# Delta rule: idle slots rebalanced, four banks for output transposes, first gathers ahead of constants, ranking without zero products

## The reference

```python
# x: (16, 512, 256)
x = layernorm(x + linear_attention(x))            # 1
x = layernorm(x + top2_of_8_experts(x))           # 2
x = layernorm(x + delta_rule_layer(x))            # 3
x = layernorm(x + composed_mlp(x))                # 4

def delta_rule_layer(x):                          # 4 heads, keys of 64, values of 128
    h = rmsnorm(layernorm(x, ln1_g, ln1_b), rms_in_w)
    q, k, v = (silu(conv4(h @ W)) for W in (Wq, Wk, Wv))      # causal, by channel
    q, k = l2norm(q) / 8, l2norm(k)
    g, beta = -exp(A_log) * softplus(h @ Wa + dt_bias), sigmoid(h @ Wb)
    for t in range(512):                          # state S: keys x values, per head
        S = S * exp(g[t])
        S = S + outer(k[t], (v[t] - k[t] @ S) * beta[t])
        o[t] = q[t] @ S
    o = rmsnorm(o, o_norm_w) * silu(h @ Wg)
    x = x + o @ Wo
    return gelu(layernorm(x, ln2_g, ln2_b) @ W2 + b2) + x

def composed_mlp(x):          # W1, W2: sums of the 32 best of 64 low-rank products
    return gelu(x @ W1) @ W2  # W1 = sum_k w_k A_k B_k, the same for W2
```

## Time and profile before

| | |
|---|---|
| three runs | 4705.86, 4717.77, 4723.58 us; median 4717.77 |
| profiled execution | 4709.05 us, its span 4707.4 us |
| busy share of the span | PE 86%, PEld 67%, DVE 53%, ACT 42%, POOL 22% |
| mean granted clock of PE | 0.907 of full speed |
| delta rule, 2080 to 4225 us | 2145 us, 46% of the span |
| mlp stages (experts, last) | PE 9 tenths busy in nearly every slice |

### The profile page before, as it was taken

How to read it: one execution, slowest core, us unless ns; L and a number is a source line. 1 busy time by engine, 2 the same in 40 slices (tenths; PEclk the granted TensorE clock), 3 DMA queues, 4 the chain that set the end, 5 groups by cost and what they waited for, 6 DMA issues and landing times. The chain is left out here.

```text
span 4707.4 us, 72598 instructions
## 1 busy us (share of the span) xinstructions
...
## 2 busy tenths in 40 slices
...
DMA packets 220431, 345.98 MB, mean 73 GB/s; under 512 B 99956, under 2 KB 171380, under 8 KB 201972
## 3 DMA queue, kind: packets, MB, share of 16 engines
...
...
## 5 line engine op out<-in xcount | busy, mean ns | idle before, releaser
L539 ACT ACTIVATE moe_rel<-moe_fc 128x512 f32<-128x512 f32 x284 | 169.6, 597 | 798.7 <-PE moe_fc L504 798.7
L504 PE MATMUL moe_fc<-moe_xT,moe_win 128*128 128x256 f32 x2272 | 504.0, 380 | 1.5 <-issue 0.8
L515 PE MATMUL moe_o<-moe_wout,moe_hT 128*128 128x256 f32 x2272 | 502.0, 379 | 0.0
L504 PEld LDWEIGHTS moe_fc<-moe_xT,moe_win 128*128 128x128 f32 x2272 | 432.9, 191 | 61.2 <-issue 2.1
L515 PEld LDWEIGHTS moe_o<-moe_wout,moe_hT 128*128 128x128 f32 x2272 | 426.3, 190 | 55.1
L563 DVE TENSOR_TENSOR moe_hT<-moe_rel 128x512 f32<-128x512 f32 x284 | 196.6, 692 | 366.5 <-ACT moe_rel L539 366.5
L1781 DVE SCALAR_TENSOR_TENSOR gdr_y<-gdr_bank,gdr_cw,gdr_y 128x511 f32<-128x511 f32 (+2 forms) x384 | 287.5, 749 | 52.6 <-ACT gdr_y L2045 29.0
L2242 PE MATMUL gdr_bank<-gdr_hT,gdr_wqkv 128*128 128x512 f32 x512 | 282.5, 680 | 21.3 <-ACT gdr_qk L2060 15.8
L572 DVE COPY moe_osb<-moe_o 128x512 f32<-128x512 f32 x71 | 49.1, 692 | 424.9 <-PE moe_o L515 424.9
L2361 PE MATMUL gdr_bank<-gdr_ident,gdr_T 128*128 128x128 f32 x768 | 132.5, 301 | 126.5 <-DMA gdr_T<-blocks_in 76.0
L693 PE MATMUL ffn_fc<-ffn_xT,ffn_win 128*128 128x512 f32 x512 | 224.0, 596 | 2.0 <-DMA ffn_win<-ffn_w 2.0
...
## 6 DMA issues: line engine op xcount, KB each, us to landing
...
```

The lines of the kernel that those rows point to most:

```text
L504: ins = nc.tensor.matmul(fc_ps[j][:, m % 2, :], win[u][:, c, m * P:(m + 1) * P], xT[:, c, :], start=(c == 0), stop=(c == DT - 1))
L515: ins = nc.tensor.matmul(o_ps[u][:, t, :], hT[u][:, k, t * P:(t + 1) * P], wout[u][:, k, :], start=(k == 0), stop=(k == FT - 1))
L539: nc.scalar.activation(rel[:, j, :, :], fc_ps[j][:], ACT.Relu).then_inc(relu_done, 1)
```

## The change

**Routing.** `edge` and the tile of zeros go. The first matmul into a bank has `start`, the last `stop`. ACT waits for the count of used steps instead of the closing `edge`.

```diff
-                    act.wait_ge(acc_done, n + 1)
+                    act.wait_ge(used, DEEP + KT)
...
-                                 start=False, stop=False, skip_group_check=True)
+                                 start=(k == 0), stop=(k == KT - 1), skip_group_check=True)
...
-                                 start=False, stop=False, skip_group_check=True)
+                                 start=(k == 0 and m % 2 == 0), stop=(k == KT - 1 and m % 2 == 1), skip_group_check=True)
```

```diff
+                gather_rows(0)
+                identity_tile(nc, pool, ident, id0, id1)
+                pool.wait_ge(id1, 1)
...
                 def period(b, u, here=False, front=False, ln=False, past=False, end=False):
-                    if ln:
-                        if later(b, -2):
-                            pool.wait_ge(got_used, b + 2)
+                    if ln and later(b, -1):
+                        pool.wait_ge(got_used, b + 2)
                         gather_rows(b + 2)
...
+                    if not later(b, -2):
+                        pool.wait_ge(got_used, 1)
+                        gather_rows(1)
+                        constants()
```

```diff
-                    sp.wait_ge(s["qd"], b * TT + 2 * pair + 2)
+                    sp.wait_ge(s["na"], b * TT + 2 * pair + 2)
...
                         invert_blocks(0, b)
+                    if end:
+                        power(b - 2, var[1][:], rstd[1][:], "tl_var", 2, "tl_rstd", TT)
...
-                    for t in (2 * pair, 2 * pair + 1):
-                        i = t % 2
-                        wait("kk", t + 1)
+                    made = lambda i, k: bank[KKB[i][k]][:].rearrange("p (w n j) -> p w n j", w=2, n=H2)
+                    for i in range(2):
+                        wait("kk", 2 * pair + i + 1)
                         for k in range(2):
-                            made = bank[KKB[i][k]][:].rearrange("p (w n j) -> p w n j", w=2, n=H2)
-                            stt(nAT[:, i, k::2, :], made[:, 0, :, :], -1.0, DT_[i][:, k::2, :], ALU.mult, ALU.mult)
-                            ins = tt(QD[t][:, k::2, :], made[:, 1, :, :], DT_[i][:, k::2, :], ALU.mult)
+                            ins = stt(nAT[:, i, k::2, :], made(i, k)[:, 0, :, :], -1.0, DT_[i][:, k::2, :], ALU.mult, ALU.mult)
+                        done("na", 2 * pair + i + 1, ins)
+                    for i in range(2):
+                        t = 2 * pair + i
+                        for k in range(2):
+                            ins = tt(QD[t][:, k::2, :], made(i, k)[:, 1, :, :], DT_[i][:, k::2, :], ALU.mult)
                         done("qd", t + 1, ins)
```

```diff
+                        if slot == 2 and end:
+                            last_sum(b - 2)
...
+                        if slot == 4 and end:
+                            last_norm(b - 2)
...
                         if slot == 6 and past:
+                            lengths_o(b - 1)
                             gated(1, b - 1)
-                        if slot == 6 and front:
+                        if slot == 7 and front:
                             lengths(b + 1)
...
                         if slot == 9 and front:
+                            rates(0, b + 1)
                             unit(b + 1)
                         if slot == 10 and front:
-                            rates(0, b + 1)
-                        if slot == 10 and ln:
-                            norm2(b + 2)
-                        if slot == 11 and front:
                             rates(1, b + 1)
                             keys_beta(b + 1)
+                        if slot == 10 and past:
+                            residual(0, b - 1)
                         if slot == 11 and past:
-                            residual(0, b - 1)
-                        if slot == 12 and past:
                             residual(1, b - 1)
-                        if slot == 12 and ln:
-                            rms(0, b + 2)
+                        if slot == 11 and ln:
+                            norm2(b + 2)
                         if slot == 13 and past:
                             norm3(b - 1)
                         if slot == 13 and front:
                             decay(b + 1, w)
                             values_beta(0, b + 1, w)
+                        if slot == 13 and ln:
+                            rms(0, b + 2)
```

```diff
+                def unit_o(h, b):
...
+                    for t in range(TT):
+                        part = o[:, t, h * VD:(h + 1) * VD]
+                        ins = a_op(part, part, ACT.Copy, scale=orr[:, t * DH + h:t * DH + h + 1])
+                    done("og", h + 1, ins)
...
+                        if past and slot == 9:
+                            turned_o(0, b - 1)
+                            turned_o(1, b - 1)
                         if front and 2 <= slot <= NP_ + 1:
                             spread_out(slot - 2, b + 1)
+                        if past and slot == 9:
+                            turned_o(2, b - 1)
+                            turned_o(3, b - 1)
+                        if past and slot == 8:
+                            unit_o(2, b - 1)
+                            unit_o(3, b - 1)
...
                             gelu(b - 2)
+                        if past and slot == 6:
+                            squares(3, b - 1)
+                        if front and slot == 6:
+                            squares_qk(b + 1)
+                        if past and slot == 7:
+                            unit_o(0, b - 1)
                         if front and slot < NP_:
                             tap(slot, b + 1)
-                        if past and slot in (9, 10):
-                            turned_o(2 * slot - 18, b - 1)
...
-                            squares(2 if slot == 3 else 3, b - 1)
+                        if past and slot == 7:
+                            unit_o(1, b - 1)
...
-                        if front and slot == 10:
+                        if front and slot == 9:
                             rates(0, b + 1, w)
                         if here and slot in (1, 2):
                             decay_keys(slot - 1, b)
-                        if past and slot == 8:
-                            unit_o(b - 1)
-                        if here and slot in (9, 11):
-                            decay_keys(2 if slot == 9 else 3, b)
-                        if front and slot == 5:
-                            squares_qk(b + 1)
-                        if ln and slot == 11:
-                            lengths_u(b + 2)
+                        if here and slot == 11:
+                            decay_keys(2, b)
+                            decay_keys(3, b)
```

```diff
+        TURN_O, MIX = (UT, YZ[0], YZ[1], SIDE), (SIDE, UT)
...
-                    wait("oTe", c) if c else wait("og", 1)
+                    wait("og", c + 1)
                     for t in range(TT):
-                        ins = tp(bank[SIDE][:, tokens(t)], o[:, t, c * P:(c + 1) * P], ident[:])
+                        ins = tp(bank[TURN_O[c]][:, tokens(t)], o[:, t, c * P:(c + 1) * P], ident[:])
...
                     wait, _ = waiter(pe, b)
-                    wait("xe", 1) if p else wait("oTe", DH)
+                    wait("oTe", DH)
                     for t in (2 * p, 2 * p + 1):
                         for c in range(DH):
-                            ins = mm(bank[SIDE][:, (t % 2) * D:(t % 2 + 1) * D], y[:, c, tokens(t)], wo_s[:, c, :],
...
                         pair, lv = slot // (LEVELS + 1), slot % (LEVELS + 1) - 1
+                        if past and slot == 10:
+                            mix_out(0, b - 1)
                         if here and lv >= BASE:
+                            if slot == 13 and past:
+                                pe.wait_ge(s["xe"], b * 2)
                             first_half(lv, 2 * pair, b)
-                        if past and slot in (10, 11):
-                            turn_o(2 * slot - 19, b - 1)
...
                         if here and lv >= BASE:
                             first_half(lv, 2 * pair + 1, b)
+                        if front and slot == 9:
+                            rates(b + 1)
+                        if past and slot == 9:
+                            if here:
+                                pe.wait_ge(s["qd"], b * TT + TT)
+                            turn_o(0, b - 1)
+                            turn_o(1, b - 1)
...
-                        if front and slot == 9:
-                            rates(b + 1)
-                        if past and slot in (9, 10):
-                            if slot == 9 and here:
-                                pe.wait_ge(s["qd"], b * TT + TT)
-                            turn_o(2 * slot - 18, b - 1)
-                        if past and slot in (11, 12):
-                            mix_out(slot - 11, b - 1)
+                        if past and slot == 9:
+                            turn_o(2, b - 1)
```

(3 more changed lines are left out.)

133 lines of the change are left out of this document (58 added, 75 removed).

## The result

| | before | after |
|---|---|---|
| median of the runs | 4711.8 us (4 runs) | 4582.5 us (4 runs, 4579.9 to 4598.9) |
| profiled execution | 4709.05, span 4707.4 | 4581.29, span 4579.3 |
| mean granted clock of PE | 0.907 | 0.924 |

The ratio is 0.9732, with a 95% interval of 0.9704 to 0.9761: 129 us faster. The prediction said 4586, range 4537 to 4664. It was added up from a median before of 4717.8 (three runs); a fourth run made that 4711.8, so what was forecast as a difference is 131 us.

A forecast was written before the change was run, and what follows sets the result against it. The delta rule was taken as bound by PE's waits and the clock lost behind them. 14 periods at −8.1 (−113), −6 for the end periods and −12.0 elsewhere gave −131.4 us: 4717.8 to 4586, range 4537 to 4664.

The forecast's parts named there:

- The copy of U: Pair 0's second merge level: ACT's squares move off this copy; −3.2 us wait and −2.6 clock, −5.8 per period.
- T and the inversion: T comes earlier in both pairs of the delta rule: A −0.5, C −3.8, D +2 us per period.
- A: Part of the period ending at pair 0's first merge level: −0.5 us (bounds −1.35 and +0.5).
- C: Pair 1's way from its key products to T: −3.8 us per period (bounds −0.8 and −4.0).
- D: From pair 1's first merge to the next key products: +2 us, clock partly lost (bounds 0 and +4).
- QD out of SP's way: SP starts behind four nAT without waiting for QD: −1.35 us in A; −0.85 in C after 0.5 for lengths.
- The power and last_sum: POOL's power leaves the place before pair 1's inversion, −1.0 us; last_sum beside pair 0's costs up to 1.2.
- Contention: In C, DVE operations with two memory inputs slow two POOL inversion steps; moving them a slot later gives −1.9 us.
- the first operation of pair 1's inversion at 0.85 us: Sign of being right: this POOL operation takes 0.85 us with no power ahead of it, not 2.06.
- The four banks: Transposes of o, all in slot 9, no longer wait for each other's copies: worth nothing inside the loop.
- The slower rival: DVE late by 5.6 us in slots 2 to 4, delaying PE's recurrence: +66 us, 4784; chance 0.07.
- Ranking, start, end: Outside the loop: ranking −10.3, delta rule's start +5, its end −5.4, last MLP −1.3; together −12.0 us.

The follow-up runs named there:

- the move alone: Kernel before with squares(3) and squares_qk moved to slot 6 of ACT, and lengths_o and lengths moved on DVE: 4629.3 us, ratio 0.9821.
- its undoing: Changed kernel with squares(3) and squares_qk put back into slot 5 of ACT: 4677.9 us, ratio 0.9921.
- the two traces: Changed kernel, and the same with o's transposes and products in one bank at their new places: 4590.0 and 4622.5 us.
- the run with them: Changed kernel with one bank and the old slots for o's transposes, their products and PE's rates: 4778.7 us, ratio 0.9967.

## Why the prediction was right, and where it wasn't

**The copy of U.** Right, shown from both sides: the move alone gives 83 us, its undoing takes 95. The term was somewhat low (−5.8 against −7.2), and its two shares came out otherwise: −3.2 for the wait and −2.6 for the clock were forecast, −1.7 and −5.6 measured. The idle time fell by less, since DVE's merge now holds PE at the same level; the clock came back wholly, 1.00 in the stretch for which I had granted half.

**T and the inversion.** Right in sign for A and C, and right that D takes a part back (its clock fell from 1.00 to 0.92), but I had the net of pair 1's half wrong (−1.8 against +0.1). Three steps failed.

The first is what part C waits for. I costed it as the way to `T`, but before the change PE waited for `T` at pair 1's first merge in none of the fourteen periods (2895.83, has no idle time). It waited for ACT: 3.0 us for a convolution's last step, 2.5 for copies of the transposed o and 2.2 for its scaling, in the mean. After the change the largest wait there is 2.24 us for ACT's `gam`, which stands behind the squares of slot 12:

```profile
3073.52 0.81 PE L2286 MATMUL gdr_bank<-gdr_ident,gdr_qk 128*128 128x128 f32 x4 [2.25 <-ACT gdr_gam L2072]
```

It is the pattern of the copy of U once more, and moving these squares wasn't tried. So the −2.4 us of part C met the sign of −3.8 by another mechanism, which no single run isolates.

The second is *QD out of SP's way*, which was to give −1.35 in A and −0.85 in C; putting it back cost 0.15 us a period. The step took a shorter way to `T` for a shorter half, where DVE's merge held pair 0's half as long. In C it didn't shorten the way to SP either: SP starts 4.5 us behind the key products against 4.3, because of `lengths`, which I had charged with 0.5 us. Rows of DVE before, and after:

```profile
2861.99 0.42 DVE L1861 SCALAR_TENSOR_TENSOR gdr_nAT<-gdr_bank,gdr_DT 128x256 f32<-128x256 f32 x1 [1.90 <-PE gdr_bank L2347]
```

```profile
3044.94 2.29 DVE L1785 TENSOR_REDUCE gdr_ssq<-gdr_sq 128x32 f32<-128x2048 f32 x1
...
3047.47 1.54 DVE L1855 SCALAR_TENSOR_TENSOR gdr_nAT<-gdr_bank,gdr_DT 128x256 f32<-128x256 f32 x4
```

The reduction began 0.5 us behind the key products' start and held `nAT` until 3.1 us behind it; before, DVE waited there and began `nAT` after 1.4 us (2861.99, with the earlier trace rows, 2860.61). *The power and last_sum* were under-rated: 1.0 us was the power itself, but its wait for `last_sum` came with it, 2.4 us together.

**Contention.** This is the third step that failed. For part C I took 1.9 us back from two operations of the inversion that run under a DVE operation of two memory inputs. Both delays stayed: 1.22 and 0.93 us before, 1.01 and 0.90 after, as means over the periods, the second now under `keys_beta` (L1823). The sign "the first operation of pair 1's inversion at 0.85 us" failed with it. For A I had charged 0.85 for `last_sum`; the delay is 0.95 in the mean. Rows of POOL, and ahead of each the DVE operation:

```profile
3005.81 1.27 DVE L1938 TENSOR_TENSOR gdr_n<-gdr_x,gdr_xa 128x1024 f32<-128x1024 f32 x1
...
3006.07 1.17 POOL L1676 TENSOR_TENSOR gdr_vblk<-gdr_vblk,gdr_tblk 64x56 f32<-64x56 f32 x1
...
3054.87 2.29 DVE L1794 TENSOR_TENSOR gdr_qk<-gdr_qk,gdr_ssq 128x2048 f32<-128x2048 f32 x1
...
3056.01 1.85 POOL L1670 TENSOR_TENSOR gdr_vblk<-gdr_wblk,gdr_low 64x256 f32<-64x256 f32 x1 [3.06 <-DMA gdr_wblk<-blocks_out]
...
3064.50 1.22 DVE L1823 TENSOR_TENSOR gdr_kb<-gdr_qk,gdr_bt 128x1024 f32<-128x1024 f32 x1
...
3064.69 1.20 POOL L1676 TENSOR_TENSOR gdr_vblk<-gdr_vblk,gdr_tblk 64x54 f32<-64x54 f32 x1
```

The step of 64x56 values takes 0.3 us elsewhere, and 1.17 under `last_sum`: 0.9 us. By the rule of the Trainium skill (SBUF — State Buffer, "Who interferes with whom": the side that comes second blocks while a VectorE instruction with two memory inputs runs) the wait is what is left of the 1.27 us when POOL comes 0.26 later: 1.0; the trace agrees. It does so in every period: of these pairs each delay is what is left of the DVE operation, less 0.12 to 0.15 us. In the period it came to little, as `T` wasn't the end of the half: with `last_sum` in slot 1 pair 0's inversion was 0.6 us shorter and the period the same. (The prediction put the full 1.23 us at some 12 us more than its own term; against the 0.85 that it had charged it is 5.)

**The four banks.** Wrong: "I cost them at nothing there". At the new places they are worth 2.2 us a period by the two traces and 32.5 us by the medians. The step that failed was that other matmuls stood between the transposes: with all four in one slot they don't, and the copies stand on ACT behind a convolution. In the places of before I can't say; the run with them carries the wait for `rates` too.

**DVE in slots 2 to 4.** The slower rival was the right mechanism in a small size: 2.6 us in pair 0's half, not 5.6, and more than paid back by 4.0 in pair 1's. The free time in slot 3 is used up, which was one of the signs of being wrong: DVE's state update has 0.2 us of idle time before it in the mean, where it had 2.9, and in this period it begins 2.6 us behind the end of its matmuls (3021.09), right behind an operation of the last norm.

```profile
3022.23 1.38 DVE L97 TENSOR_SCALAR gdr_x<-gdr_n,gdr_agg,gdr_rstd 128x256 f32<-128x256 f32 x4
3023.65 1.43 DVE L1892 SCALAR_TENSOR_TENSOR gdr_S<-gdr_S,gdr_gam,gdr_bank 64x128 f32<-64x128 f32 x4
```

A convolution and then the merge that PE waits for stand behind it.

**Ranking, start, end.** −10.3 was exact. The start cost +7.4, not +5: nothing later absorbed the wait for `ready`, and the last power ended only 4 us earlier behind POOL's first instruction (32.1 against 36.1), not 5.7. At the end the wait for the first transposes fell by 3.5 us (11.79 to 8.29), transposes and copies from 7.4 to 6.4, and the second product's 0.88 went: −5.4, the forecast. The last MLP's first matmuls came 3.1 us sooner, not 1.3, as its input doesn't stand behind the copy of the spare rows any more either.

That the total met the forecast so closely (131 us against 129) is partly luck, by these errors' signs: the banks, the squares and the last norm gave more than I said, `QD`, `lengths`, the contention and the start less.
